# Five hand-written instruction orders replaced, and a value copy cut into 2048-byte rows, in a two-stage attention kernel

## The reference, cut to what matters

```python
h = _layernorm(x) * (1 + ca) + sa
x = x + ga * attention(h, Wq, Wk, Wv, Wo, bo)          # causal, once
h = _layernorm(x) * (1 + cb) + sb
for i in range(6):                                     # the "local" part
    s = shift_tokens(h)
    q, k, v = split(s @ Wqkv[i])                       # 16 heads of 64
    q, k = rotary(l2norm(q) * q_scale[i]), rotary(l2norm(k) * k_scale[i])
    h = local_attention(q, k, v, window=32) @ Wo[i] + h
    h = ffn_layer(shift_tokens(h), ...) + h            # layernorm, 682 wide, gelu
x = x + gb * h
```

## Time and profile before

| | |
|---|---|
| Median of the three timed executions | 3510.96 us (3510.58 to 3515.58) |
| Span of the profiled execution, first to last instruction | 3495.1 us |
| Local part | 48 batches, from about 680 us |
| PE, POOL, DVE, ACT busy, share of the span | 95%, 83%, 84%, 71% |

### The profile page before, as it was taken

The page is one execution under the profiler, slowest core; times in us unless marked ns, Lnnn a source line. Parts: engine busy times, 40 slices in busy tenths (PEclk is TensorE's granted clock), DMA queues, the critical chain, the costliest instruction groups (busy, mean ns, idle before and its releaser), DMA issues.

```text
span 3495.1 us, 158019 instructions
## 1 busy us (share of the span) xinstructions
PE 3309.7 (95%) x69988; PEld 1936.2 (55%) x69988; DVE 2951.4 (84%) x3104; ACT 2468.4 (71%) x3349; POOL 2907.1 (83%) x2483
## 2 busy tenths in 40 slices
PE   7999999779999999999999999999999999999997
PEld 4666666445555555555555555555555555555553
DVE  6888888688888988888888889888998889988873
ACT  5777777556777767777677777676877777767764
POOL 3665555588999989999899999898999999989993
PEclk9999999999999999999999999999999999999997
DMA  1000000154645545545455454555554554545452
GB/s 67 5 5 5 5 5 5 44 119 102 143 114 130 120 115 126 131 112 127 113 126 127 106 137 110 129 120 121 120 135 105 142 124 109 140 108 134 102 124 62
DMA packets 163861, 347.33 MB, mean 99 GB/s; under 512 B 32876, under 2 KB 42352, under 8 KB 153840
## 3 DMA queue, kind: packets, MB, share of 16 engines
q1 hardware_dynamic: 163184, 337.23, 40.9%
HBM read 24.62 MB, written 4.19 MB: 8 GB/s over the span
## 4 chain that ended last, share of the span: by engine, by line
PE 70%; DVE 11%; POOL 6%; issue 6%; ACT 4%; SPq 2%; DMA 1%; DVEq 0%; POOLq 0%; ACTq 0%
PE psA L697 29%; PE psB L697 23%; PE psB L559 8%; PE psA L559 6%; PE psB L754 3%; DVE h L1338 3%; DVE pt L1237 1%; SPq L490 1%; PE psA L754 1%; DVE negm L1342 1%; DVE sum L1349 1%; DVE ts L1330 1%; DVE h L1320 1%; DMA kf<-h 1%; POOL sq L1443 1%
## 5 line engine op out<-in xcount | busy, mean ns | idle before, releaser
L1410 POOL TENSOR_TENSOR pt<-wk,pt 128x256 f16<-128x256 f32 (+3 forms) x256 | 368.1, 1455 | 288.7 <-ACT pt L939 199.0
L1443 POOL TENSOR_TENSOR sq<-sq 128x512 f32<-128x512 f32 x384 | 488.5, 1281 | 79.6 <-ACT sq L1022 78.2
L1438 POOL TENSOR_TENSOR h<-h,ts 128x512 f32<-128x512 f32 x384 | 499.8, 1302 | 1.2 <-DVE ts L1330 1.2
L1439 POOL TENSOR_TENSOR h<-h,ts 128x512 f32<-128x512 f32 x384 | 497.1, 1295 | 0.0
L1338 DVE TENSOR_TENSOR h<-h,psB 128x1024 f32<-128x1024 f32 x288 | 337.8, 1215 | 57.1 <-PE psB L697 55.5
L1463 POOL TENSOR_TENSOR pb<-pb,rc 128x1024 f32<-128x1024 f32 x192 | 366.3, 1908 | 8.8 <-DVE rc L1351 8.8
L1320 DVE TENSOR_TENSOR h<-psA,t_rot 128x1024 f32<-128x1024 f32 x192 | 234.2, 1220 | 72.7 <-ACT sq L1022 65.7
L697 PE MATMUL psA<-kf,qf 64*32 64x64 f32 x18432 | 251.2, 224 | 22.0 <-issue 21.6
L697 PEld LDWEIGHTS psA<-kf,qf 64*32 64x32 f32 x18432 | 191.5, 106 | 124.8 <-issue 124.4
L1320 DVE TENSOR_TENSOR h<-psB,t_rot 128x1024 f32<-128x1024 f32 x192 | 233.4, 1216 | 26.2 <-ACT sq L1022 20.4
L1022 ACT ACTIVATE sq<-psA 128x1024 f32<-128x1024 f32 x192 | 197.0, 1027 | 63.7 <-PE psA L697 63.5
(11 more groups left out here) (368 smaller groups left out, 10242.0 us busy)
## 6 DMA issues: line engine op xcount, KB each, us to landing
qf<-h SPq DMA_DIRECT2D x768, 136.0 KB
kf<-h SPq DMA_DIRECT2D x768, 136.0 KB, 2.5
vev<-vo SPq DMA_DIRECT2D x288, 256.0 KB
vev<-vo SPq DMA_DIRECT2D x96, 192.0 KB
stage<-wqk SPq DMA_DIRECT2D x24, 256.0 KB, 5.0
stage<-wvl SPq DMA_DIRECT2D x12, 256.0 KB, 4.1
stage<-wof SPq DMA_DIRECT2D x12, 256.0 KB, 5.5
xb<-xt SPq DMA_DIRECT2D x8, 256.0 KB, 7.9
```

Of the source, the lines that this page charges most:

```text
L1410: e.tensor_tensor(pt[g][pr][:, :, 1, o:o + w], wk[(slot_of(s)[0] - 1) % SLOTS][:, :, 0:w], pt[g][pr][:, :, 0, o:o + w], ALU.subtract).then ...
L1438: e.tensor_tensor(halves_of(h, 0), halves_of(h, 0), t[1], ALU.subtract)
L1439: e.tensor_tensor(halves_of(h, 1), halves_of(h, 1), t[0], ALU.add).then_inc(ended["ad"])
L1443: e.tensor_tensor(sqb[c][:, 0, :], sqb[c][:, 0, :], sqb[c][:, 1, :], ALU.add).then_inc(ended["qa"])
```

## The change

All five strings are rewritten. Whole batches are shifted too, but what counts is the order inside one batch: there SP keeps its order, and each other engine keeps most of its own: some 10 tokens of 33 to 58 stand in another place or another bank. Two banks get a more exact wait: behind `pj` it waits for whichever of `tc` and `ts` stands last, behind `la` for whichever of `lq` and `lw`. The rows of `vev` are 32 bytes longer than their 2048 bytes of data, so that a copy into it can't run over the rows as one piece: its packets become 2048 bytes. The work of every engine is the same; PE has 43 semaphore waits fewer.

```diff
 TENSOR = (
-    "pv000:B+1 ng10+1 pv001+1 ss1:Dl+1 sc110:A+1 tp01:C+1 sc113+1 sc111+1 sc112+1 pj00:B+2 pv010:D+1 ng11+1 pv011+1 "
...
+    "vp10:A+1 ng11+1 pv010:D+1 pv011+1 fo:Bl tp10:C+1 vp11:A+1 bc10:C+1 bc11:B+1 f2:D+1 f0:A+1 pv100:C+1 pv101+1 pj01:D+2 "
...
-LAST = {"tp": "te", "op": "rs", "pj": "ts", "ss": "nr", "vp": "ve", "la": "lw",
-        "lb": "ln", "f": "fm", "fo": "fr"}
+LAST = {"tp": "te", "op": "rs", "ss": "nr", "vp": "ve", "lb": "ln", "f": "fm", "fo": "fr"}
...
-        vev = sb("vev", [128, NT, 2, 4, DH])
+        vev_rows = sb("vev", [128, NT, 2 * 4 * DH + 8])
+        vev = vev_rows[:, :, 0:2 * 4 * DH].rearrange("p t (f x d) -> p t f x d", f=2, x=4)
...
+        def later(steps, a, b):
+
+            return max(a, b, key=steps.index)
...
+                    elif k == "pj":
+                        e.wait_ge(*done(*later(vector_walk, ("tc", *at), ("ts", *at))))
+                    elif k == "la":
+                        e.wait_ge(*done(*later(scalar_walk, ("lq", *at), ("lw", *at))))
...
-            e.memset(vev.rearrange("p t f r d -> p (t f r d)"), 0.0).then_inc(s_init)
+            e.memset(flat(vev_rows), 0.0).then_inc(s_init)
```

More of the change, by code:

```diff
@@ L126 @@
 TENSOR = (
[5 rows of a table removed]
[5 rows of a table added]
 )
 SCALAR = (
[3 rows of a table removed]
[4 rows of a table added]
 )
 VECTOR = (
[4 rows of a table removed]
[4 rows of a table added]
 )
 GPSIMD = (
-    "gl1 lx+1 nw1+1 pn10+1 cs1+1 fl+1 ct1+1 xl+2 ad13+1 pn11+1 qa00+2 ad00+2 qa01+2 qa02+2 qa03+2 ad01+2 ad02+2 gl0+1 "
-    "nw0+2 cs0+2 ct0+2 ad03+2 qa10+2 ad10+2 pn00+2 qa11+2 qa12+2 ad11+2 pn01+2 qa13+2 ad12+2 gl2+1 "
+    "qa02+3 xl+3 qa03+3 ad01+3 ad02+3 nw0+3 cs0+3 ct0+3 qa10+3 ad10+3 ad03+3 pn00+3 gl0+2 ad11+3 qa12+3 gl1+2 pn01+3 "
+    "qa11+3 qa13+3 ad12+3 lx+3 nw1+3 pn10+3 cs1+3 fl+3 ct1+3 ad13+3 pn11+3 qa00+4 ad00+4 gl2+3 qa01+4 "
 )
 SYNC = (
-    "st6 st7 dm00+1 dm01+1 dm02+1 dm03+1 st5+1 vd0+1 dm10+1 dm11+1 st4+2 dm12+1 dm13+1 vd1+1 "
+    "st4+4 dm10+3 dm11+3 dm12+3 dm13+3 st6+4 vd1+3 dm00+4 dm01+4 dm02+4 dm03+4 st5+4 st7+4 vd0+4 "
 )
```

## The result

The changed kernel takes 3552.44 us in the median of four executions (3543.91 to 3560.47), the kernel before 3513.27 us (3510.58 to 3521.09). The ratio is 1.0112, interval 1.0086 to 1.0137: **slower by 39 us**, where I had forecast 30 us less.

The account below looks back on a forecast made before the run. PE was taken as the limit, with POOL close behind. Gains of 34 us (stretches) and 4 (packets), less 8 (layer changes), gave 30 us less: 3465 us in the profiled execution, 3481 timed; 8 in 10 for 3448 to 3530.

Parts of the forecast that it names:

- I expect their waits to stay, 0 in the sum: PE's waits for instruction blocks: dense stretches remain as long in instructions, so no change, 0 us.
- First stretch, POOL: From the end of op to bc10: POOL's chain to ct1 ends at 2300.05 instead of 2300.85, 0.8 us sooner.
- First stretch, PE: From the end of op to bc10: PE gains 0.6 us a batch, between 0 and 0.8.
- That `sc100` can't come over 0.2 us sooner: In the first stretch, copies hold sc100 to about 0.2 us before its present time; the rest becomes a wait.
- Second stretch: From bc10 to the next op: 0.1 us a batch gained, between 0 and 0.3; the ss0-to-ct0 chain limits it.
- Packets: Copies to vev in 2048-byte packets let instruction blocks in sooner: 4 us less over the run, between 0 and 20.
- Changes of layer: At five layer changes w2h stands ahead of all four bm, delaying bm10: 8 us more, between 0 and 29.
- the first one: Rival: POOL's f_gl2 ahead of three sq makes ss0 wait, so the kernel is slower, 3530 in the middle; chance 0.22.
- Blocks stop being waited for: Rival: half of PE's 80 us of idle time goes too, 40 us more gain, about 3440; chance 0.10.
- The rule on block boundaries: Cited skill rule for instruction fetch: crossing a block boundary is mostly hidden, so nothing would be won there.
- the 34 that I had summed: Gain of the new orders over both stretches: 0.7 us a batch times 48 batches, 34 us.

Follow-up runs that it names:

- q3: The changed kernel with vo multiplied first in each pv group and the late waits for vev's copy and te put on matmuls; ratio 0.9915 to the kernel before.
- p1: The kernel before with only the rows of vev padded, so that copies go in packets of 2048 bytes; ratio 0.9994 to the kernel before.
- r1: q3 with w2h (ws0) put back behind bm12, where it stood before; 2 us less than q3 by the ratios, intervals overlapping.
- q1: The kernel before with the waits for vd and bm in pv100 changing places; ratio 1.0138 to the kernel before, 48 us more.
- r2: q3 with the waits for the copies to qf and kf put on mask matmuls at the head of sc; 4 us less than q3, intervals overlapping.
- q4: The kernel before with q3's edit of the waits in the pv groups; ratio 0.9963 to the kernel before, 13 us gained.
- q2: The changed kernel with vp10 put back behind pv011, as before; ratio 1.0083 to the kernel before.

## Why the prediction was wrong

- **The step that failed** is "I expect their waits to stay, 0 in the sum", about instruction blocks. I had counted how dense PE's instructions lie and found no change; what changed was when a block is asked for. "Issue" rose from 38.4 to 92.2 us. Of the moved tokens I had not looked at `vp10` and the copy to `vev` at all. Had I, I would have found slack, since `bm` ends later: that holds for the data and not for the instructions. The tell-tale was in the earlier trace rows: a block was still in flight when PE came to it, so it had been asked for too late. I asked what lay ahead of it in the queues and not what the sequencer had waited for.
- **First stretch, POOL**: the sum is right, what it was compared with is not. In the batch at 2362.09 `pn01` starts 14.59 us after `op` (13.60 in the earlier trace rows) and `ct1` ends 30.83 after it (31.76), 0.9 sooner; forecast 0.8. From the start of `pn01` to the end of `ct1` it is 16.24 us (my sum: 16.25), and the pause before `cs1` is gone:

```profile
2376.68 1.90 POOL L1472 TENSOR_TENSOR pb<-pb,rc 128x1024 f32<-128x1024 f32 x1
...
2390.50 0.67 POOL L1462 TENSOR_TENSOR n_a<-n_a,n_c 128x256 f32<-128x256 f32 x1
2391.13 1.16 POOL L1482 TENSOR_TENSOR f_cl<-f_c,f_ch 128x512 f16<-128x512 f32 x1
2392.25 0.67 POOL L1467 TENSOR_TENSOR n_b<-n_a,n_c 128x256 bf16<-128x256 f32 x1
```

  But the pause of 0.85 us, which my sum took away from every batch, is not in every batch before. In the one from 2721.42 POOL has none, and `ct1` ends 30.86 us after `op`, no later than in the new order:

```profile
2748.00 1.91 POOL L1463 TENSOR_TENSOR pb<-pb,rc 128x1024 f32<-128x1024 f32 x1
2749.86 0.68 POOL L1453 TENSOR_TENSOR n_a<-n_a,n_c 128x256 f32<-128x256 f32 x1
2751.61 0.67 POOL L1458 TENSOR_TENSOR n_b<-n_a,n_c 128x256 bf16<-128x256 f32 x1
```

  In the trace before, that pause is over 0.3 us in 18 of 43 batches and 0.34 us in the mean; with the new orders it is gone in all but one. So 0.8 a batch should have been about 0.3, an estimate from these means. I had worked it out from one batch, and that one was late: PE waits 0.7 us for blocks in it. Over the run the median `ct1` comes 0.72 us later than before, 32.35 after `op`, and in q3 it is back at 31.59, 0.04 sooner than before.
- **First stretch, PE**: 0.6 forecast, 0.72 between the two batches (32.86 to 32.14), but the one of the earlier trace rows has 0.7 us of waits for blocks in this stretch; so it confirms nothing. That `sc100` can't come over 0.2 us sooner was wrong: it starts 9.99 us after `op` in the middle instead of 10.89. The last copy had landed 0.95 us ahead of it in the middle before (0.28 in the batch of the earlier trace rows), and it lands 0.5 sooner now. `sc100` does wait for the copies (10.0 us of `kf<-h` against 1.5).
- **Second stretch**: 0.1 forecast, 0.05 between the same two batches (23.10 to 23.05), too little to tell. The chain from `ss0` to `ct0` keeps its length, 8.6 us in the middle before, after and in q3.
- **Packets**: -4 us forecast, -2 measured (p1), inside the measurement.
- **Changes of layer**: +8 forecast. The five waits for `bm` went from `tp11` (15.6 us) to `pv100` (12.5 us), and r1 says 2 us: nothing that can be told from zero.
- **The rivals**: the sign was that of the first one, the mechanism was not: `ss0` is not held up by POOL. "Blocks stop being waited for" named the right resource with the wrong sign. By the page "Perfetto Trace Analysis" of the Trainium skill (section "Per-engine timelines"), a sequencer-only instruction waits for its semaphores on the sequencer, while a matmul waits in a queue behind it and the sequencer goes on; q1 agrees, and shows the price, 48 us, which the page doesn't tell. The rule on block boundaries that the prediction cited ("mostly hidden") holds here only in part: 92.2 of 2500 us are "issue" in the changed kernel, 38.4 in the one before, and 34.2 are left in r2, where the late waits are on matmuls.
- **How far the order's gain goes**: q3 is at the 30 us of the forecast, but q4 shows that 13 of them come from the waits. The five orders themselves are worth about 17 us (0.9963 to 0.9915; 5 to 28 by the two intervals), half of the 34 that I had summed, and near the 0.3 a batch above. The profiles can't take it apart: in the rows PE's busy time falls from 55.14 to 54.55 us a batch between q4 and q3 (its share of the 2500 us times the batch), and the idle time takes it back, 1.57 to 2.19. The two profiled executions are only 5 us apart (3476.10 and 3471.46), since q4's is the fastest of its ten.

## What to carry to other kernels

Where an engine runs through many short instructions, ask of each wait ahead of a dense group not only whether it ends last, but where it stands: the first wait in code rode on the matmul, the others in an instruction that holds up the sequencer. Put the latest wait on the matmul, and further late ones on later matmuls that first need them; here that was worth 0.4% in the old order and 2.0% in the new one. A single buffer whose copy is just in time deserves distrust even if nobody waits for it in the profile. And when batches of one kernel differ by 4 us at equal work, look at the worst one before judging the order by the mean, and at several before making one of them the yardstick.

## What the runs showed of the hardware that I had not expected

**A gap costs more than its length.** After the gap that ended at 1463.85 PE works on, and 1.4 us later the clock is granted at half. The windows of the gap and of that time:

```profile
1461.42:1463.84 2.42, 0.20 (x16) 0.13 (x9) 1.56 (x2) 0.50 (x1) 2.42 (x3) 1.00 0.48 106
1465.30:1468.70 3.40, 3.40 (x14) 2.26 (x13) 3.01 (x3) 2.05 (x3) 1.27 (x1) 0.50 0.95 218
```

That is 1.2 GHz instead of 2.4, and the matmuls of 512 columns start every 0.43 us instead of every 0.22:

```profile
1464.32 0.38 PE L702 MATMUL psB<-xs1l,wqh 128*128 128x512 f16 x1
1464.54 0.38 PE L702 MATMUL psB<-xs1h,wqh 128*128 128x512 f16 x1
...
1467.62 0.63 PE L702 MATMUL psA<-xs1l,wqh 128*128 128x512 f16 x1
1468.05 0.63 PE L702 MATMUL psA<-xs1h,wqh 128*128 128x512 f16 x1
```

Such stretches occur 4 times between 900 and 3400 before, 25 times after (92 us in all), 5 times in q3. Of the 25, 24 begin within 1.5 us of the end of a gap of 1.3 to 2.8 us. They go with the long gaps, not with the sum: q2 has 78.2 us of "issue" but only 6 gaps of 2 us and more, where after has 19, and 5 such stretches. Not every long gap is followed by one (3 of the 19 are not). PE's busy time per batch shows it: 55.29 us before, 55.60 after, 54.55 in q3 with the same order as after. So of the 2.00 us by which a batch of the changed kernel is longer than one of q3, 0.95 is idle time and 1.05 is PE working more slowly.

**A swap of two waits, 48 us.** In the rows before, PE never waits for the one (`vd`), and at most 0.6 us in all for the other (`bm` at `pv100`). A profile shows who was late for the data; that the instructions themselves were asked for late, it shows only as "issue".
